# A joint reciprocal of two sets of softmax denominators, moved from VectorE to GpSimd as a power of minus one

## The reference, cut to what matters

```
xn = layernorm(x)
q = xn@Wq+bq ; latent = xn@Wl+bl ; k = latent@Wk+bk ; v = latent@Wv+bv       # 16 heads of 8
attn = softmax(q k^T * 8**-0.5) ; a = (attn v) @ Wo + bo
f = batchnorm(xn@fWq+fbq)                                                    # 8 heads of 2 x 16
s0, s1 = l2norm(f halves) . l2norm(keys)                                     # 32 scores each
top 4 of each, 4 x 4 sums, softmax over the 16, index i0*32+i1
out = sum over the 16 of  up[idx] * gelu(down[idx] . xn) * weight
result = x + a + out
```

## Time and profile before

| | us |
|---|---|
| median of 3 runs | 319.01 |
| lowest and highest of these | 318.46, 320.83 |
| the profiled execution, whole | 320.12 |
| its span, first to last instruction | 318.3 |
| mean granted TensorE clock | 0.989 of full speed |

### The profile page before, as it was taken

The page is one execution under the profiler, slowest core; times in us unless marked ns, Lnnn a source line. Parts: engine busy times, 40 slices in busy tenths (PEclk is TensorE's granted clock), DMA queues, the critical chain, the costliest instruction groups (busy, mean ns, idle before and its releaser), DMA issues.

```text
span 318.3 us, 9910 instructions
## 1 busy us (share of the span) xinstructions
PE 297.8 (94%) x3179; PEld 167.3 (53%) x3179; DVE 302.2 (95%) x1356; ACT 285.3 (90%) x519; POOL 268.6 (84%) x509
## 2 busy tenths in 40 slices
PE   8999999998899999999999999999999999999896
PEld 3555555343355555555465555555555555465445
DVE  7799999889799999999999999999999999999994
ACT  3799995997889999999999999999999999998991
POOL 7289895962689999999999999999999999999940
PEclk9999999996899999999999999999999999999999
DMA  4856666518650405051512133331514040000001
GB/s 132 224 150 190 172 184 165 139 35 112 69 97 8 100 6 118 11 110 33 92 48 74 53 70 81 39 81 42 102 19 119 5 117 22 3 21 0 22 20 33
DMA packets 45888, 24.83 MB, mean 78 GB/s; under 512 B 5452, under 2 KB 45708, under 8 KB 45836
## 3 DMA queue, kind: packets, MB, share of 16 engines
q1 hardware_dynamic: 45836, 24.20, 33.6%
HBM read 15.54 MB, written 8.39 MB: 75 GB/s over the span
## 4 chain that ended last, share of the span: by engine, by line
POOL 36%; DVE 20%; PE 20%; issue 14%; ACT 5%; SPq 2%; DMA 1%; POOLq 1%; ACTq 0%
POOL prod L1362 8%; DVE negm L1110 6%; POOL r_sb L1350 6%; PE bank L783 5%; POOL z_sb L1414 4%; DVE r_sb L1098 4%; POOL order L1416 3%; POOL on L1327 3%; DVE inverse L1088 2%; POOL cm L1418 2%; PE SI L604 2%; PE bank L754 2%; PE bank L632 2%; ACT Eb L430 1%; DVE top L1137 1%
## 5 line engine op out<-in xcount | busy, mean ns | idle before, releaser
L1110 DVE TENSOR_REDUCE negm<-SI 128x4 f32<-128x1024 f32 x128 | 152.5, 1212 | 4.0 <-PE SI L693 3.9
L487 ACT ACTIVATE Eb<-SJ 128x1024 f32<-128x1024 f32 x117 | 119.4, 1021 | 4.6 <-PE SJ L734 3.2
L754 PE MATMUL bank<-Eb,vhat 128*18 128x256 f32 x1024 | 67.8, 382 | 3.9 <-ACT s_sb L401 3.5
L1362 POOL TENSOR_TENSOR prod<-r_sb,a 128x1024 f32<-128x1024 f32 x28 | 53.6, 1913 | 0.0
L734 PE MATMUL SJ<-QS,KS 50*128 50x256 bf16 x484 | 47.8, 275 | 4.4 <-ACT Eb L487 3.7
L693 PE MATMUL SI<-KS,QS 48*128 48x256 bf16 x512 | 50.6, 274 | 0.8 <-DVE negm L1110 0.2
L1137 DVE MAX8 top<-s_sb 128x8 f32<-128x32 f32 x480 | 47.3, 176 | 0.5 <-ACT s_sb L401 0.5
L754 PEld LDWEIGHTS bank<-Eb,vhat 128*18 128x18 f32 x1024 | 24.0, 97 | 30.5 <-issue 10.0
L1098 DVE MATCH_REPLACE8 r_sb<-top,s_sb 128x32 f32<-128x32 f32 x240 | 39.6, 175 | 0.0
L783 PE MATMUL bank<-cst,prod 128*128 128x128 f32 x240 | 32.8, 280 | 2.4 <-POOL prod L1370 0.3
L693 PEld LDWEIGHTS SI<-KS,QS 48*128 48x128 bf16 x512 | 20.5, 95 | 25.0 <-issue 17.3
(11 more groups left out here) (223 smaller groups left out, 621.1 us busy)
## 6 DMA issues: line engine op xcount, KB each, us to landing
qk_parts<-parts SPq DMA_DIRECT2D x48, 128.0 KB, 2.4
QS<-qk_parts SPq DMA_DIRECT2D x32, 96.0 KB
KS<-qk_parts SPq DMA_DIRECT2D x32, 96.0 KB
x_sb<-L_attn_x SPq DMA_DIRECT2D x8, 256.0 KB, 3.5
QS<-qk_parts SPq DMA_DIRECT2D x32, 64.0 KB
KS<-qk_parts SPq DMA_DIRECT2D x32, 64.0 KB
out<-ysb SPq DMA_DIRECT2D x16, 128.0 KB, 2.6
QS<-qk_parts SPq DMA_DIRECT2D x32, 32.0 KB
```

Of the source, the lines that this page charges most:

```text
L487: A(Eb[:, n % 4, :], SJ[:, :], ACT.Exp).then_inc(s["ex"], 1)
L754: last = mm(psO[32 * c:32 * c + 2 * VC, (q % 2) * S:(q % 2 + 1) * S], vhat[:, v0:v0 + 2 * VC], Eb[:, (2 * g + c // 2) % 4, e0:e0 + S], sta ...
L1110: V.tensor_reduce(negm[:, bb % 2, :, :, pr].rearrange("p t e -> p e t"), SI[slot % 2][:, :].rearrange("p (e t j) -> p e t j", e=2, j=S), a ...
L1362: TT(prod[:, t, :, :, :], r_sb[:, hs, 0:NK].unsqueeze(2).to_broadcast([P, FH, TOP, NK]), a0[:, hs, :].unsqueeze(3).to_broadcast([P, FH, TO ...
```

## The change

The instruction at L1088 goes, with its five lines of waits. GpSimd gets a `tensor_tensor` with the operation `pow` in its place: base `denominators`, exponent a column of -1.0 stretched over the 48 elements. That column is a fourth column of the tile `eps`, set once by a GpSimd memset at the start. The new instruction stands between GpSimd's `gated(b - 1)` and `normalised(b - 1)` (slot k = 3 of GpSimd's order), with the same waits plus one for the memset, and signals the same semaphore `rd`.

```diff
-        eps = sb("eps", [P, 3]); less = eps[:, 1:2]; last_row = eps[:, 2:3]
+        eps = sb("eps", [P, 4]); minus_one = eps[:, 3:4]; less = eps[:, 1:2]; last_row = eps[:, 2:3]
...
-            def inverses(b):
-
-                dve.wait_ge(s["ct_ev"], b)
-                dve.wait_ge(s["fp"], b + 1)
-                dve.wait_ge(s["fa"], b)
-                if b >= 2:
-                    dve.wait_ge(s["on"], b - 1)
-                V.reciprocal(inverse[:, :], denominators).then_inc(s["rd"], 1)
-
...
-                    if quarter == 1 and i == REPLACED[1] + 1 and b >= 1:
-                        inverses(b)
...
+            V.memset(minus_one, -1.0).then_inc(s["minus"], 1)
...
+            def inverses(b):
+
+                pool.wait_ge(s["minus"], 1)
+                pool.wait_ge(s["ct_ev"], b)
+                pool.wait_ge(s["fp"], b + 1)
+                pool.wait_ge(s["fa"], b)
+                if b >= 2:
+                    pool.wait_ge(s["on"], b - 1)
+                TT(inverse[:, :], denominators, minus_one.to_broadcast([P, BT * H + BT * FH]), ALU.pow).then_inc(s["rd"], 1)
...
                         gated(b - 1)
+                        inverses(b)
                         normalised(b - 1)
```

More of the change, by code:

```diff
@@ L198, in program @@
         names = (
-            "w0 w w2 zeros eps stats aggr std rstd nm xn xn0 xT xnT vzero vzero2 vone kone pad "
+            "w0 w w2 zeros eps stats aggr std rstd nm minus xn xn0 xT xnT vzero vzero2 vone kone pad "
             "wl wl_ev wkv wkv_ev q q_ev k k_ev v v_ev f f_ev f_st "
```

## The result

The changed kernel takes 444.59 us (median of 4 runs, 443.11 to 445.93) against 318.89 us before: the ratio is 1.393, with a 95% interval of 1.388 to 1.399. The prediction was 328.7 us with a range from 318.2 to 340.4. It had the sign, and it was far off in size.

The account below looks back on a forecast made before the run. VectorE was taken as the bound, GpSimd within 0.35 us per block; the move makes GpSimd the longer, adding 14 × (0.96 − 0.27) = 9.7 us to the median 319.01, giving 328.7 us, range 318.2 to 340.4.

Parts of the forecast that it names:

- What d is: Step estimating the new GpSimd power's duration from other instructions' rows, since the trace shows no power; it took 0.96 us.
- d: Duration of the new 48-element power on GpSimd, once per block; taken as 0.96 us, the middle of 0.71 and 1.22.
- the prediction's own formula: Added time is 14 × (d − 0.27) us, from GpSimd's longer path per block; 9.7 us forecast.
- two functions, each as dear as that division: Upper estimate for the power on GpSimd, as logarithm and exponential at 0.51 us each plus 0.20 fixed: 1.22 us.
- slow power: Rival: each element costs twenty to forty multiplications on GpSimd, d 1.8 to 3.4 us, kernel 340.4 to 363 us; chance 0.26.
- no wait for the new instruction's input: ScalarE's copy of the denominators ends at 186.61, GpSimd arrives at 186.83; a margin of 0.22 us that should hold.
- 0.08 us for the dependent start: GpSimd's division of the heads, needing the power's result, starts 0.08 us after the power ends.
- a power at the price of a product: Rival: the power costs GpSimd the same as a multiplication, d 0.28 us, kernel 319.1 us; chance 0.28.
- a gain of more than about 1%: Rival: GpSimd has slack the trace doesn't show, so VectorE's saved 5.5 us come through, 313.5 us; chance 0.03.
- GpSimd's slack: GpSimd's only recurring wait per block, for the joint reciprocal, gives 0.35 us of slack and a serial path of 14.61 us.
- VectorE's work per block: Without the reciprocal, VectorE's path per block falls by 0.39 us, from 14.96 to 14.57 us.
- the list of what would show it: Signs in the profile after, chiefly a block of 14.69 + d us; any other length means unseen GpSimd waits or slack.

Follow-up runs that it names:

- e1: Kernel before, with single powers of 8 to 256 elements and a multiplication behind GpSimd's last work; 48 elements side by side took 8.00 us.
- e5: Changed kernel with 32 otherwise useless TensorE matmuls ahead of its wait for the divided heads; 429.11 us, ratio 1.346 to the kernel before.
- e2: Changed kernel with the power replaced by a multiplication of the same operands, same place and waits; ratio 1.0034 to the kernel before, 1.1 us slower.
- e3: Kernel before without the joint inverse on any engine, GpSimd multiplying with the denominators themselves; ratio 0.992, 2.7 us faster.
- e9: Kernel with VectorE inverting 32 attention denominators and GpSimd the filter's 16 by a power right behind the division of the heads; 360.92 us, ratio 1.131.

## Why the prediction was wrong

**The step that failed is "What d is".** The direction and the way of reckoning stand, but the term that carries the sum was mis-sized: d was taken as 0.96 us and is 8.06. Put into the prediction's own formula, 14 × (8.06 − 0.27) = 109.1 us, it gives 428.0. The bounds were drawn from the ratio of a division to a product on VectorE, 6.4, and an assumption of twenty multiplications for each element, with forty named as the far end. The measured price is 95 multiplications per element (e1): the step from VectorE's division to "two functions, each as dear as that division" had them at 0.51 us each, and the 7.7 us of the power beyond its fixed part are some 3.8 us for each. The ratio of 1.96 between GpSimd's and VectorE's elementwise addition in the Trainium skill (GPSIMD Engine Reference, Elementwise — side-by-side cycle accounting) would have given an estimated 0.89 us, nine times too little. It speaks of an addition, and the rows that the prediction set beside it as "the same pair", 1913 against 1220 ns, are of a multiplication. The rival "slow power", held at 0.26, is the case that came, though its own numbers ended at 363 us. No row of the trace of before excluded 8 us, and the prediction said so; the range then ended at a count of multiplications that nothing measured.

**What was missing altogether is the clock**: 15.5 us of the 125.7 (e5). The prediction said that the other engines would wait for GpSimd, and left their speed afterwards alone. The account is then: 109.1 us by the formula, 15.5 us for TensorE's clock, 1.1 us left over of 125.7. Of the 1.1 us, 14 × 0.06 = 0.8 us would be GpSimd's path, which had been read 0.06 us per block too short.

**Right**, with their runs: no wait for the new instruction's input; 0.08 us for the dependent start; all of d on the path, nothing hidden (e5); a power at the price of a product giving no change (15.04 us per block in e2 against 14.97, 319.1 forecast, 1.1 us slower measured); a gain of more than about 1% excluded even for a free inverse (e3). **A little off**: GpSimd's slack, 0.35 us by one block of the trace, is 0.29 by the mean of e2; VectorE's work per block, forecast as 14.57 us, is 14.66 in e3, 14.80 in e2 and 14.79 in the changed kernel, for a reason that was not traced, and without weight for the time. **Wrong in the list of what would show it**: the block is 23.91 us and not 14.69 + 8.06 = 22.75, and the prediction had named this as the sign of something it did not see. What it took that for, waits or slack of GpSimd, did show (1.09 us for VectorE's MAX8), with the clock as its cause.

## What to carry to other kernels

When an operation moves to an engine whose trace does not show it, the neighbouring operations of that engine price at most the fixed part of the instruction, not its arithmetic (here not even that, 0.20 us against 0.37): if one unknown price decides the sign or the size, measure that one instruction first, at two lengths. A fully busy engine that is relieved gives next to nothing when another has only 0.3 us of slack per 15 us block; leaving the whole step out (e3) shows the ceiling at once, here about 1%. And a stall that lets TensorE stand still is paid twice if an engine without slack waits for TensorE right behind it: look at the granted clock of the stretch after the stall, not only at the stall.

## What the runs showed of the hardware that I had not expected

- A power on GpSimd costs 0.37 us and 0.159 us per element (8 to 256 elements), the same for exponents −1, 2, −0.5 and 1 within 0.01 us, the same for 1, 16 and 128 partitions, and at most 0.05 us of 8 more at a stride of 9 elements.
- TensorE's granted clock fell to 0.52 behind 7.84 us of idle time, to 0.50 for 4.8 us behind 3.03 us, and in five of eight blocks of e9 behind a wait of about 1.9 us (0.52 from 228 to 231 us), while the other three, with the same wait, kept 1.00. It stayed at 1.00 when 32 or 26 otherwise useless matmuls filled the same time. In the changed kernel they gain 3.5%.
